# One 8 KB row per transfer in place of four 2 KB pieces, for 27 of the 30 table blocks of a two-layer graph network

## What is computed

```python
# layer 0: relational attention, 4 heads of 64
h = relu(layernorm(x))
feat_all = einsum('ni,rhid->rnhd', h, conv_weights)      # 8 relations per node
e = leaky_relu(el + er)                                  # per edge and head
alpha = softmax of e over the edges of one destination
x = x + segment_sum(alpha * feat_all[type, src], dst) + h_bias
# layer 1: relational convolution
h = relu(layernorm(x))
W = einsum('rb,bio->rio', comp, basis)                   # 8 matrices 256 x 256
h_all = einsum('ni,rio->nro', h, W)                      # 8 rows of 256 per node
agg = segment_sum(h_all[src, type], dst)
g = gelu(agg + h @ loop_w + h_bias + h)
x = x + layernorm(g) * gamma + beta
```

## Time and profile before

| | |
|---|---|
| median of 3 runs | 3184.79 us (3178.91 to 3190.22) |
| the profiled execution: its own time | 3185.23 us |
| its span, first to last instruction | 3183.6 us |
| layer 0's edge groups | about 230 to 1740 us of the span |
| layer 1's edges | about 1800 us to the end |
| mean granted TensorE clock | 0.767 of full |
| DMA traffic | 399.40 MB, mean 125 GB/s |

### The profile page before, as it was taken

How to read it: one execution, slowest core, us unless ns; L and a number is a source line. 1 busy time by engine, 2 the same in 40 slices (tenths; PEclk the granted TensorE clock), 3 DMA queues, 4 the chain that set the end, 5 groups by cost and what they waited for, 6 DMA issues and landing times.

```text
span 3183.6 us, 27639 instructions
## 1 busy us (share of the span) xinstructions
PE 1972.1 (62%) x8172; PEld 1422.7 (45%) x8172; DVE 1525.6 (48%) x3205; ACT 680.2 (21%) x1278; POOL 1990.5 (63%) x2108
## 2 busy tenths in 40 slices
PE   7973557776777777767777726555445444544455
PEld 6962444554555555555555415333333323332334
DVE  6743555665666656656757404232223323332235
ACT  4634114333324323324322200000000000000000
POOL 5746665666666666666666365666676667666763
PEclk9985678888888888888878957777666666666667
DMA  8545344554544554554554432333333333333332
GB/s 228 213 176 180 103 128 129 154 144 139 155 141 140 149 147 140 149 147 140 148 150 118 138 93 74 94 95 91 96 98 96 94 92 103 91 95 90 103 95 60
DMA packets 167122, 399.40 MB, mean 125 GB/s; under 512 B 49279, under 2 KB 75360, under 8 KB 159294
## 3 DMA queue, kind: packets, MB, share of 16 engines
q0 software_dynamic: 93920, 257.77, 30.0%
q1 hardware_dynamic: 73054, 139.85, 12.8%
HBM read 321.61 MB, written 75.86 MB: 125 GB/s over the span
## 4 chain that ended last, share of the span: by engine, by line
another core or an unknown queue 31%; DVE 29%; PE 18%; issue 12%; POOL 7%; DVEq 2%; DMA 0%; ACT 0%; SPq 0%; ACTq 0%; POOLq 0%
PE PB L1945 9%; POOL rows L902 7%; DVE Z L1414 6%; PE PB L1900 4%; DVE OHZ L1404 4%; DVE ACC L1378 3%; DVE ACC L1386 3%; DVE oh L1626 3%; PE PB L1963 1%; DVE ERM L1395 1%; PE PB L2088 1%; DVEq L1355 1%; DVEq L1365 1%; PE PB L2135 0%
## 5 line engine op out<-in xcount | busy, mean ns | idle before, releaser
L872 POOL DMA_INDIRECT Z<-tab,KI x996 | 949.6, 953 | 588.1 <-issue 277.4
L902 POOL DMA_INDIRECT rows<-tab,KI x938 | 886.7, 945 | 500.2 <-issue 276.9
L1963 PE MATMUL PB<-rows,oh 128*128 x1992 | 668.0, 478 | 696.4 <-issue 529.5
L1963 PEld LDWEIGHTS PB<-rows,oh 128*128 128x128 f32 x1992 | 473.2, 241 | 891.0 <-issue 821.9
L1386 DVE TENSOR_TENSOR ACC<-ACC,PB 128x256 f32 x498 | 209.6, 421 | 963.3 <-remote 872.8
L1945 PE MATMUL PB<-Z,OHZ 128*128 128x260 f32 x1992 | 606.5, 463 | 73.3 <-DVE ACC L1378 51.3
L1945 PEld LDWEIGHTS PB<-Z,OHZ 128*128 128x128 f32 x1992 | 448.8, 235 | 177.3 <-issue 85.2
L1378 DVE TENSOR_TENSOR ACC<-ACC,PB 128x260 f32 x498 | 211.7, 425 | 217.6 <-remote 117.7
L1414 DVE TENSOR_TENSOR Z<-Z,PB 128x2048 f32<-128x2048 f32 (+1 forms) x124 | 281.5, 2270 | 0.0
L2088 PE MATMUL PB<-w,ht 128*128 128x512 f32 x448 | 202.7, 606 | 19.0 <-ACT ht L1818 17.1
L1880 ACT ACTIVATE ACC<-ACC 128x256 f32<-128x256 f32 x30 | 10.4, 406 | 890.1 <-DVE ACC L1386 636.3
(11 more groups left out here) (354 smaller groups left out, 1858.7 us busy)
## 6 DMA issues: line engine op xcount, KB each, us to landing
OHZ<-dlt SPq DMA_DIRECT2D x31, 1024.0 KB
tab<-st SPq DMA_DIRECT2D x120, 256.0 KB
tab<-Z SPq DMA_DIRECT2D x24, 1040.0 KB
Z<-tab,KI POOLq DMA_INDIRECT x996
rows<-tab,KI POOLq DMA_INDIRECT x938
TD<-typ SPq DMA_DIRECT2D x31, 256.0 KB
tab<-Z SPq DMA_DIRECT2D x5, 1024.0 KB
xn<-xb SPq DMA_DIRECT2D x30, 128.0 KB
```

What stands on the lines that cost most here:

```text
L872: pool.indirect_dma_start(rows0(g)[:, k, :], None, tab0, at).then_inc(d_fe[g % 2], 16)
L902: pool.indirect_dma_start(ROWS1[:, k:k + D], None, tab1, at).then_inc(d_r[c // 8 % (RING // 4)], 16)
L1963: last = pe.matmul(place1(v), OH1[:, v // 8 % 2, 2 * (v % 8) + i, :], rows_[:, D * i:D * i + D], start=(i == 0), stop=(i == 1))
```

## The change

For blocks 0 to 26 `store_table` waits for the fourth quarter only and issues one DMA of 128 rows of 8 KB. The completion is counted on `d_st[0]` alone, so ScalarE waits on `d_st[0]` before it overwrites the first quarter, and not before the others. Blocks 27 to 29 keep four stores and four counters. The sums that the final waits expect follow from it. No computation and no byte moved is different.

```diff
+        def stored(j, r):
+            return 16 * (min(r, LATE) * (j == 0) + max(r - LATE, 0))
...
             def store_table(r):
                 t = block_rows(sp, SYE, r, tab1p)
+                if r < LATE:
+                    sp.wait_ge(s_ev, moved(r, 3))
+                    sp.dma_start(t, ST1[:, :, :].rearrange("p j f -> p (j f)")).then_inc(d_st[0], 16)
+                    return
                 for j in range(4):
                     sp.wait_ge(s_ev, moved(r, j))
                     sp.dma_start(t[:, 512 * j:512 * j + 512], ST1[:, j, :]).then_inc(d_st[j], 16)
...
             for j in range(4):
-                sp.wait_ge(d_st[j], 16 * NB)
+                sp.wait_ge(d_st[j], stored(j, NB))
...
             for j in range(4):
-                pool.wait_ge(d_st[j], 16 * NB)
+                pool.wait_ge(d_st[j], stored(j, NB))
...
             def move_quarter(r, j):
                 ac.wait_ge(s_mm, product_of(r, j))
-                if r:
-                    ac.wait_ge(d_st[j], 16 * r)
+                if r > LATE or r and j == 0:
+                    ac.wait_ge(d_st[j], stored(j, r))
                 ac.activation(ST1[:, j, :], quarter_bank(r, j)[:, :], ACT.Copy).then_inc(*o.of(s_ev))
```

## The result

| | before | after |
|---|---|---|
| median | 3182.30 us (3173.77 to 3190.22, 11 runs) | 3197.44 us (3185.18 to 3210.23, 11 runs) |
| the profiled execution, its span | 3185.23, 3183.6 us | 3199.41, 3197.8 us |
| start of the first gather of layer 1 | 1799.87 us | 1814.50 us |

The account below looks back on a forecast made before the run. GpSimd's gathers and three pauses a group were taken to bound layer 0. Terms of 0, 0 and 6 us (0.24 us a group, 26 groups) took 3185.23 to 3179 us, a gain of 0.2%; range 3152 to 3197 us.

Parts of the forecast that it names:

- What bounds the kernel: GpSimd's gathers in layer 0: 40.0 us of a 48.05 us group, the rest three pauses; layer 1 out of reach.
- The removed waits of SyncE: SyncE in 27 blocks, three waits and issues fewer: free 4 to 5.7 us earlier, nobody waits for it, 0.
- The moved start: Transfer of the first three quarters starts only with the fourth; nobody waits for the store, 0.
- The kept bytes: Same 1 MB per block in 30% fewer q1 packets: 0.24 us a group, 6 us over 26 groups.
- the bound from above: Layer 0 groups without any store take 47.24 us against 48.05, so the store is worth at most 0.8 us a group.
- the second rival: Pause moves from k = 4 to a later gather: 0.8 us a group, 21 us gained, 3164 us; chance 0.22.
- The first rival: No pause at k = 4 any more, no price elsewhere: 77 us gained, 3108 us; chance 0.11.
- The third rival: Layer 0 gathers starve behind the store's burst: 1.25 us a group, 33 us slower, 3218 us; chance 0.20.

Follow-up runs that it names:

- late4: Kernel before, its four transfers of 2 KB rows all issued after the fourth quarter is moved; ratio 1.0010 (1.0001 to 1.0019).
- after_5: The changed kernel run again, unedited, on a 3180-us chip; 3204.75 us against 3177.43 before, ratio 1.0074 (1.0051 to 1.0097).
- the waits by hand: GpSimd made to wait at k = 4, 16, 24 for its own earlier gathers; kernel before 2998.53 us, changed kernel 2975.90 us.

## Why the prediction was wrong

**What bounds the kernel** held: the loss is 14.6 us of layer 0, all in GpSimd's pauses, and layer 1 takes the same.

**The removed waits of SyncE, 0,** held: SyncE's issue ends 2.25 us before the k = 3 gather and not 3.37 us behind it, 5.6 us earlier, and nobody starts earlier for it.

**The moved start, 0,** held on the 2720-us chips (late4 1.0010), and not where GpSimd waits for landings: there a later start gains 0.9 to 1.1 us a group by the profiles. I had weighed only who waits for the store and not which gathers it is let in ahead of.

**The kept bytes, 0.24 us a group:** the 22 steady groups of the first two profiles are 0.31 us shorter, 6.9 us for my 6. That the number fits may be luck. Nothing shows that fewer packets bring it, as the start and the issues changed with them, and the later steady groups of after_5 (16 to 22 and 24 to 31) take 47.9 us, only 0.1 below the 48.03 of groups 7 to 31 before.

**The failed step** is the bound from above, with the pauses of GpSimd taken as something that can only shrink or stay: "Group 3's k = 24 gather comes 47.24 us after group 2's", taken as what a group costs with no store, and in the second rival as a gain of 0.8 us a group when "the pause moves from k = 4 to a later gather". The pause did move, in group 29, to k = 8. It cost 17.8 us over three groups: the group with the moved pause is cheap or a little dear (47.24 and 47.32 before, 49.29 after), and the next pays (52.14 and 56.82 before, 60.43 after), because TensorE's flip comes 5 us later in it and is counted 10.1 us later still. The row of group 4 stood in the same list, and I used its pauses at k = 24 but not its 7.28 us at k = 4. A price has to be read over the pair. The second rival had the mechanism and the wrong sign, and the range, 3152 to 3197, had no slip in it; one makes 3179 + 18 = 3197, so that the median came out at the very end of the range is the one slip, and no burst. (The end I gave stood for a burst of 0.5 us a group, which makes 3185 + 13 = 3198. The 65 us between block 26's store and the next were 51, 1727.47 to 1778.60; nothing hung on them.)

**The first rival** (one issue ends the standstill, 3108 us) was wrong, and my argument against it right: VectorE's restart stays 3.40 us behind the k = 3 gather with one issue of 0.34 us. I had noticed that the matmuls waited for "are listed as over by 965.3" and soon after, and didn't ask when they were counted: `select`'s at 971.93. The trace of before held that.

**The third rival** (3218 us by a starving of 1.25 us a group) had the sign and not the cause. In 965 to 968 us q1 has more of the engines and q0 less than in the same stretch of before (75.1% and 20.4% against 32.1% and 44.6%):

```profile
q1 hardware_dynamic: 125, 0.89, 75.1%
q0 software_dynamic: 59, 0.19, 20.4%
```

The burst is there as said, and the steady groups are shorter all the same. These shares agree with what I had cited of the Trainium skill ("DMA: Bandwidth & Descriptors", Queues, rings and completion order), that each DMA engine turns between the queues by whole packets. VectorE's restart hangs on the count of `select` there and on no landing, which is why I take the burst to have cost nothing; the waits by hand show the price once somebody waits.

**What is shown and what stays open.** Shown: in both sets of runs at 3180 us the loss is made of slips, three groups in one profile and five in the other, and in the one profile of the kernel before none of groups 7 to 31 slips; the price of a slip lies in a flip that TensorE makes late and that is counted later still; where there are no pauses, there is no loss. Open: what tips a steady group, that is, what lets GpSimd go on 0.7 to 1.5 us earlier than usual at k = 4 of the group ahead of the dear one (1.65, 2.40 and 2.35 us of pause in groups 29, 12 and 22, where 3.1 is usual). SyncE's issue lies 2.61 us before the k = 3 gather in group 12 of after_5, which slips, and 2.62 in group 11, which doesn't; TensorE's last product ends 0.03 us behind that gather and 0.06 us before it. That the changed kernel slips more often than the one before rests on two profiles against one and on the medians of the two sets. The parts of the change were not tried on a 3180-us chip, so which of them brings the slips, start, rows or issues, isn't known. Nor is why TensorE's counts come late there while GpSimd gathers, and on the 2720-us chips don't.

No version beat the kernel before on a chip as it is.

## What to carry to other kernels

When the trace of before holds a place where a pause sits elsewhere, read its price up to the point where the rhythm is back, never from one period alone. Look in a steady pattern for the irregular periods at its start: they show what the change can tip it into. Where a wait ends long after its producer is listed as over, look up when the semaphore was counted, and what else stopped just before. And a burst of DMA beside gathers cost here by its start against the next wait; a price of its larger rows could not be told from the scatter.

## What the runs showed of the hardware

The same kernel takes 3177 to 3182 us on some chips and 2718 to 2725 us on others, with a group of layer 0 at 48 and at 40 us, and GpSimd's gather itself is 0.95 us with 0.30 us between on both. The pauses differ, and so does what they hang on: TensorE's flips and selects are counted 0.01 us behind their listed ends in all sixteen profiles of the one kind, and up to 10.3 us late in the four of the other, when GpSimd has been issuing gathers for some time. The profile of the kernel before also holds 13087 records of semaphore updates from a 3180-us chip and 43050 from a 2720-us chip, for the same program; whether updates or only records are missing isn't shown, and those of `select` are complete in both. A change can be worth nothing on the one and lose 0.45 to 0.74% on the other, so a verdict holds for the kind of chip that it was measured on.
